# The four token stages of layer 0 run as one pipeline instead of four fenced stages

## The reference

```python
x = L0_attn_hidden_states                      # 4 batches x 2048 tokens x 256
x = x + 0.5 * _L0_ffn_ref(_layernorm(x), ...)  # layer 0
x = x + _L0_attn_ref(_layernorm(x), ...)
x = x + 0.5 * _L0_ffn_ref(_layernorm(x), ...)  # layer 1

# _L0_ffn_ref, per token
logits = flat @ router_w.T
topk_scores, topk_idx = jax.lax.top_k(logits + router_bias, TOPK)   # TOPK = 2
topk_scores = jax.nn.softmax(topk_scores, axis=-1)
hidden = jax.nn.silu(gate_all) * up_all        # 16 experts
out = jnp.einsum('nk,nkd->nd', combine, down_all)
sh_hidden = jax.nn.silu(flat @ sh_gate.T) * (flat @ sh_up.T)
out = out + sh_hidden @ sh_down.T
```

## Time and profile before

| | us |
|---|---|
| median of 3 runs | 2016.77 |
| lowest and highest of them | 2015.26 and 2021.91 |
| the profiled execution, whole | 2013.89 |
| its span in the trace | 2012.2 |
| PE busy, share of the span | 1480.4, 74% |
| DVE busy, share of the span | 1047.0, 52% |
| POOL busy, share of the span | 876.3, 44% |

### The profile page before, as it was taken

How to read it: one execution, slowest core, us unless ns; L and a number is a source line. 1 busy time by engine, 2 the same in 40 slices (tenths; PEclk the granted TensorE clock), 3 DMA queues, 4 the chain that set the end, 5 groups by cost and what they waited for, 6 DMA issues and landing times.

```text
span 2012.2 us, 35562 instructions
## 1 busy us (share of the span) xinstructions
PE 1480.4 (74%) x11274; PEld 1247.8 (62%) x11275; DVE 1047.0 (52%) x3253; ACT 617.5 (31%) x1254; POOL 876.3 (44%) x1108
## 2 busy tenths in 40 slices
PE   4797787999967779578767779698674447799650
PEld 3787677988854548455654559587543327698540
DVE  4657546544434755556734766243553547474332
ACT  2333223444423323233212323244321103244220
POOL 4563486655532200210272006655135463756656
PEclk9897798999976889688877889799786767799775
DMA  4732224556541122210231021356223352256555
GB/s 116 225 104 65 84 79 126 167 164 157 161 136 43 48 74 74 81 39 24 90 121 43 27 74 63 107 160 156 84 64 110 105 157 77 87 156 176 147 146 170
DMA packets 166002, 215.71 MB, mean 107 GB/s; under 512 B 18800, under 2 KB 143856, under 8 KB 165872
## 3 DMA queue, kind: packets, MB, share of 16 engines
q0 software_dynamic: 32256, 90.22, 17.0%
q1 hardware_dynamic: 87920, 79.74, 12.3%
q10 hardware_dynamic: 45696, 44.05, 6.6%
HBM read 119.56 MB, written 94.37 MB: 106 GB/s over the span
## 4 chain that ended last, share of the span: by engine, by line
PE 53%; DVE 14%; POOL 13%; issue 10%; DMA 4%; ACT 4%; another core or an unknown queue 2%; ACTq 0%; DVEq 0%; POOLq 0%; SPq 0%
PE bank L1444 8%; PE bank L1455 7%; PE bank L1594 7%; PE bank L1457 6%; PE bank L1456 6%; PE bank L1515 4%; DMA out<-normalised_rows 3%; POOL queries_high L739 2%; POOL normalised_rows L655 2%; POOL gathered_last_results L655 2%; DVE bn_stats L1042 2%; POOL rows_and_results L722 2%; PE bank L1846 2%; DVE score_maxima L1328 2%
## 5 line engine op out<-in xcount | busy, mean ns | idle before, releaser
L722 POOL DMA_INDIRECT rows_and_results<-normalised_by_token,rows_of_slots x336 | 319.7, 952 | 215.4 <-PE bank L1444 131.5
L655 POOL DMA_INDIRECT gathered_results<-slot_results,slot x128 | 122.0, 953 | 389.4 <-DVE combined_rows L1278 282.8
L1226 DVE TENSOR_TENSOR rows_transposed_low<-bank,rows_transposed_high 128x512 fp32r<-128x512 f32 x168 | 116.0, 691 | 270.2 <-ACT rows_transposed_high L812 178.6
L1455 PE MATMUL bank<-expert_gate_up_high,rows_transposed_high 128*128 x672 | 210.3, 313 | 47.1 <-DVE rows_transposed_low L1226 27.1
L737 POOL TENSOR_SCALAR keys_high<-iota,place_in_page_of_choice 128x128 fp32r<-128x128 f32 x96 | 57.6, 600 | 330.1 <-DVE place_in_page_of_choice L1165 322.7
L1456 PE MATMUL bank<-expert_gate_up_low,rows_transposed_high 128*128 x672 | 194.3, 289 | 0.0
L1457 PE MATMUL bank<-expert_gate_up_high,rows_transposed_low 128*128 x672 | 194.1, 289 | 0.0
L1594 PE MATMUL bank<-expert_down,hidden_work 128*128 x672 | 186.6, 403 | 0.5
L1455 PEld LDWEIGHTS bank<-expert_gate_up_high,rows_transposed_high 128*128 128x128 f32 x672 | 132.8, 198 | 60.0 <-issue 58.5
L1455 PE MATMUL bank<-rows_transposed_high,shared_gate_up_high 128*128 128x256 f32 x512 | 159.1, 311 | 0.3 <-DVE hidden_work L1001 0.3
L1444 PE MATMUL bank<-identity,hidden_work 128*128 128x128 f32 x464 | 96.8, 308 | 78.0 <-ACT hidden_work L766 29.8
(11 more groups left out here) (277 smaller groups left out, 3754.9 us busy)
## 6 DMA issues: line engine op xcount, KB each, us to landing
slot_results<-rows_and_results ACTq DMA_DIRECT2D x168, 256.0 KB
partial_sums<-rows_and_results SPq DMA_DIRECT2D x96, 256.0 KB, 2.1
rows_and_results<-partial_sums SPq DMA_DIRECT2D x72, 256.0 KB, 4.3
normalised_by_token<-normalised_rows SPq DMA_DIRECT2D x64, 256.0 KB, 2.5
rows_and_results<-in_L_attn_hidden_states SPq DMA_DIRECT2D x32, 256.0 KB, 3.3
normalised_rows<-partial_sums POOLq DMA_DIRECT2D x24, 256.0 KB
out<-normalised_rows POOLq DMA_DIRECT2D x24, 256.0 KB, 2.7
rows_and_results<-normalised_by_token,rows_of_slots POOLq DMA_INDIRECT x336
```

The source lines that it names most:

```text
L655: gp.indirect_dma_start(into[:, t, k, :], None, ys[part], bass.IndirectOffsetOnAxis(ap=slot[:, b, k, 2 * i + t:2 * i + t + 1], axis=0))\
L722: gp.indirect_dma_start(rows[:, i % NS, t, :], None, norm_d, bass.IndirectOffsetOnAxis(ap=listed[:, page:page + 1], axis=0))\
L1226: dve.tensor_tensor(flat(xt_l[:, k]), bank[k][:], flat(xt_h[:, k]).bitcast(F32), ALU.subtract)\
L1455: pe.matmul(out_, lh, rh, start=first, stop=False)
```

## The change

Stages 1 to 3 become `chained`. Their engines no longer wait at a fence. The stage before them (`ph["next"]`) issues the first work of the next batch inside its own last turns: statistics and norm of pairs 0 and 1 on DVE at turn 6, `apply` of both pairs on ACT at turns 7 and 8, `turn` of pair 0 on PE and `high` on ACT at turn 8, `low` of pair 0 and the norm of pairs 2 and 3 on DVE at turn 9. A chained stage has three norm groups instead of two. The third one (pairs 4 to 7) stands at its turn 2.

The slot computation of a batch moves too. Its chunks stand at turns 0, 2, 3, 4 and 5 of the stage; in stage 3 chunk 3 stands at turn 3. `list_slots` of the stage's slots is left to turn 3 of the following stage, with the last 14 of 32 `invert` matmuls in that stage's turns 0 to 3. Only stage 3 still ends with its own list. The ranks go to `bank[1]` instead of `bank[5]`, so `turn(3)` has to wait for the two DVE operations that read them. SP loads a pair of the next batch one turn earlier.

```diff
@@ the phases
+            ph["chained"] = bool(ph["kind"] == "T" and ph["n"] and phases[ph["n"] - 1]["kind"] == "T")
+            ph["next"] = phases[ph["n"] + 1] if ph["kind"] == "T" and phases[ph["n"] + 1]["kind"] == "T" else None
+        def groups_of(ph):
+            return ((0, 2), (2, 4), (4, PB)) if ph["chained"] else LN_GROUPS[ph["kind"]]
@@ SP, tokens
-                    if after["kind"] == "T" and i >= 2:
-                        load_when_stored(i - 2)
+                    if after["kind"] == "T" and i >= 1:
+                        load_when_stored(i - 1)
@@ ACT, tokens
-                apply(0)
-                apply(1)
+                if not ph["chained"]:
+                    apply(ph, 0)
+                    apply(ph, 1)
                 for i in range(PB + 1):
-                    if i < PB:
-                        high(i, i % NS)
+                    if i < PB and not (i == 0 and ph["chained"]):
+                        high(ph, i)
+                    if i == PB and ph["next"]:
+                        high(ph["next"], 0)
                     if i:
-                        tanh(i - 1, (i - 1) % NS)
+                        tanh(i - 1)
                     if i + 2 < PB:
-                        apply(i + 2)
+                        apply(ph, i + 2)
+                    if i >= PB - 1 and ph["next"]:
+                        apply(ph["next"], i - PB + 1)
@@ DVE, tokens
                 for i in range(PB + 2):
-                    if i < PB:
-                        low(i, i % NS)
-                    if i == 0:
-                        for n in range(5, PB):
-                            rows_statistics(n)
-                        layer_norm(ph, 2)
-                    if hosted and i < ROUTE_CHUNKS:
-                        next(hosted)
+                    if i < PB and not (i == 0 and ph["chained"]):
+                        low(ph, i)
+                    if i == PB + 1 and ph["next"]:
+                        low(ph["next"], 0)
+                    if ph["chained"]:
+                        if i == 0:
+                            next(hosted)
+                        if i == 2:
+                            next(hosted)
...
+                    if ph["chained"]:
+                        if i in (1, 2):
+                            rows_statistics(ph, 2 + 2 * i)
+                            rows_statistics(ph, 3 + 2 * i)
+                        if i == 2:
+                            layer_norm(ph, 4)
+                        if i == 3:
+                            next(hosted)
+                            if listed_late:
+                                list_slots(listed_late)
+                        if i == (4 if ph["next"] else 3) or i == 5:
+                            next(hosted)
+                    if ph["next"]:
+                        if i == PB - 2:
+                            rows_statistics(ph["next"], 0)
+                            rows_statistics(ph["next"], 1)
+                            layer_norm(ph["next"], 0)
+                        if i == PB:
+                            weight_differences()
+                            rows_statistics(ph["next"], 2)
+                            rows_statistics(ph["next"], 3)
+                        if i == PB + 1:
+                            layer_norm(ph["next"], 2)
@@ PE, tokens
+                    if i == 3 and ph["chained"]:
+                        r = ph["hosts"]
+                        pe.wait_ge(route.sem, r["route"] + ROUTE_PICKED + ROUTE_RESET * r["start"] + 2)
...
+                    if i == PB and ph["next"]:
+                        turn(ph["next"], 0)
+                    if i == 2 and ph["chained"]:
+                        pe.wait_ge(tr_low.sem, tr_low.done(ph["t"] + 1))
+                        ranks(ph["hosts"], bank[1])
...
+                    if listed_late and i < 4:
+                        invert(listed_late, INVERTED_LATE[i], INVERTED_LATE[i + 1])
...
+INVERTED_CHAINED = (0, 0, 3, 8, 13, 18, 18)
+INVERTED_LATE = (18, 18, 23, 28, 32)
+INVERTED_LAST = (0, 0, 4, 9, 14, 20, 32)
@@ every engine, at the start of a phase
-                fence(pe, "pe", ph["n"])
+                if not ph["chained"]:
+                    fence(pe, "pe", ph["n"])
```

More of the change, by code:

```diff
@@ L540, in _ @@
                     load_tokens(ph, range(NS))
+                if ph["chained"]:
+                    tokens(ph)
+                    continue
                 if ph["n"]:
@@ L1033, in tokens @@
                         choose(i - 1, (i - 1) % NS)
[L1034 to L1037 removed]
+                    if ph["chained"]:
+                        if i in (1, 2):
[8 more added lines that the diff above has]
+                        if i == (4 if ph["next"] else 3) or i == 5:
+                            next(hosted)
+                    if ph["next"]:
[9 more added lines that the diff above has]
+                            layer_norm(ph["next"], 2)
+                if not ph["next"]:
+                    if hosted:
+                        list_slots(ph["hosts"])
+                    weight_differences()
                 dve.drain().then_inc(phase_done["dve"].sem, 1)
@@ L1429, in _ @@
             for ph in phases:
-                fence(dve, "dve", ph["n"])
+                if not ph["chained"]:
+                    fence(dve, "dve", ph["n"])
                 {"T": tokens, "E": experts, "C": combine, "A": attention}[ph["kind"]](ph)
@@ L1517, in down_ @@
                     m.then_inc(dn_pe.sem, 1)
+                listed_late = phases[ph["n"] - 1]["hosts"] if ph["chained"] else None
+                inverted_by = INVERTED_BY if not ph["chained"] else INVERTED_CHAINED if ph["next"] else INVERTED_LAST
                 for i in range(PB + 2):
-                    if i < PB:
-                        turn(i, i % NS)
+                    if i < PB and not (i == 0 and ph["chained"]):
+                        turn(ph, i)
+                    if i == PB and ph["next"]:
[3 more added lines that the diff above has]
+                        ranks(ph["hosts"], bank[1])
                     if 1 <= i <= PB:
@@ L1525, in tokens @@
                         down_(i - 2, (i - 2) % NS)
+                    if listed_late and i < 4:
+                        invert(listed_late, INVERTED_LATE[i], INVERTED_LATE[i + 1])
                     if ph["hosts"]:
-                        if i == 1:
-                            ranks(ph["hosts"])
+                        if i == 1 and not ph["chained"]:
+                            ranks(ph["hosts"], bank[5])
                         if i >= 4:
-                            invert(ph["hosts"], INVERTED_BY[i - 4], INVERTED_BY[i - 3])
+                            invert(ph["hosts"], inverted_by[i - 4], inverted_by[i - 3])
                 pe.drain().then_inc(phase_done["pe"].sem, 1)
```

70 lines of the change are left out of this document (38 added, 32 removed).

## The result

The changed kernel takes 1998.97 us in the median of four runs (1992.5 to 2000.01), the kernel before 2016.01 us in the median of four (2014.29 to 2021.91). The ratio is 0.9911, with a 95% interval of 0.9893 to 0.993. The forecast was 2000 us.

The account below looks back on a forecast made before the run. PE was taken to set the pace over most of the span, with some 20 us per stage filling and draining. Gains of 30.9 us less 6.5, 4.5 and 5.6 gave 14.3, forecast 2000 us, range 1987 to 2014.

Parts of the forecast that it names:

- the mark: Start of ACT's exponential that waits for stage 3's list; the wait was forecast to end near 286 us.
- the three costs: Stage 0 with its crossing 6.5 us, builds beside norms and chunks 4.5, falls of PE's clock 5.6.
- Clean pipeline: Rival: short stalls leave the clock high, builds don't touch DVE; gain 20 to 28 us, 1987 to 1994; chance 0.20.
- The stage laid out on paper: A chained stage takes 57.6 us between last silus; stage 1 gains 10.4 us, stage 2 gains 13.7.
- Stage 3: POOL's 32 builds set its end, 77.8 us after stage 2's last silu; gain 6.8 us.
- Stage 0: Added statistics and a norm of 5.4 us lose 4 us inside, 2.5 more at the crossing to stage 1.
- Builds beside the norm: POOL's builds stretch norms to 3.6 us at six places, and chunks 0 to 2 of stages 2 and 3: 4.5 us.
- The rival in which DVE waits for each build: A norm takes 7.4 us; the kernel becomes 14 us slower than before, near 2028; chance 0.07.
- The clock: PE falls to 1.2 GHz after stalls of some 3 us: two falls in three stages, 2.8 us each, 5.6 in all.
- My sign for it: More than three stretches of granted clock 0.5 in stages 1 to 3 would price the clock higher.
- The sum: Clean gain 30.9 us less costs of 6.5, 4.5 and 5.6 makes 14.3 us.
- The signs: Last silus of stages 0 to 3 near 81, 140, 200 and 259 us, with 58 to 62 us between them.

Follow-up runs that it names:

- the yardstick: The changed kernel run once more, unchanged, on the second chip: 1993.73 us, ratio 0.988 to the kernel before.
- e9: Changed kernel, but in stage 3 POOL does the first 22 of 32 builds and DVE the last 10: 1996.94 us, ratio 0.9849 to the kernel before.
- e4: Changed kernel, but POOL fills the low halves of the expert weights by one-input copies, not subtractions: 1994.87 us, ratio 0.9852 to the kernel before.
- e3: Changed kernel with the inversions of stages 1 and 2 one turn later: 1993.13 us, ratio 0.9891 to the kernel before.
- e8: Changed kernel with the inversions of stages 1 and 2 and the third norm each one turn later: 1989.41 us, ratio 0.9855.
- e5: Changed kernel with fences back and no next-batch work begun early; late list, moved chunks and three norm groups kept: 2021.72 us, ratio 0.9986.

## Why the prediction was right

The time was right to about 1 us, and so was the mark (286 forecast, 286.71 measured). That is closer than the steps deserve, since two of the three costs were mis-sized in opposite directions, and so it is partly luck. On the second chip the same change saves 22.9 us (ratio 0.988), more than the 17 forecast and at a time, 1993.7, that I had given to the rival *Clean pipeline*, though the clock falls there as well. (That rival's gain was added up wrongly: 5 to 10 us less of costs make 19 to 24 us, not 20 to 28.)

- **The stage laid out on paper.** Clean, it was 57.6 us for gaps of 11.8, 3.6, 10.9, 4.5 and then 26.8. Stage 2 after has 11.8, 3.7, 10.7, 7.8 and then 30.4 (5.9, 11.4, 6.4, 6.7), 64.4 in all. The first three gaps are right to 0.2 us each, with the queue order and durations of the earlier trace rows alone. That each of them fits is luck, since the yardstick has 11.7, 5.2 and 9.1; that their sum fits isn't, 26.3 on paper against 26.2 and 26.0, and 26.9 in stage 3. In stage 1 it is 29.9. Pair 3 is too slow by 3.3 us and pair 5 by about 5, of which 1.7 is waiting for the builds; behind these lie the two stretches at 1.2 GHz, some 3.3 us each.
- **Stage 3.** Its end is set by POOL, as forecast: 78.6 us from the end of stage 2's last silu, where I had 77.8. e9 shows it directly, since giving a third of the builds to DVE moves the list by 7.4 us while the silus stay. The clock's fall from 236 to 241 costs nothing here: DVE works without a pause from 234.51 until chunk 3 is done at 242.6.
- **Stage 0.** The 4 us inside the stage were 5.7 at its last silu; a fall of the clock (78 to 81) stands in front of it. The 2.5 at the crossing show in stage 1, whose first three gaps are 3.6 us over the lay-out. The norm took 5.1 us for a forecast of 5.4 (5.5 by the last row). e4 takes this cost away and ends stage 0 at 77.1.
- **Builds beside the norm: the wrong term.** I took 4.5 us, with a norm of 3.6 at six places. Builds stand beside only four norms of stages 1 to 3. These take 3.0 to 3.4 us, the one from 134.61 to 137.87 3.3, hardly above the 2.9 of the earlier trace rows: 1.3 us together. The third groups take 3.0 us each, with twice the elements and no build beside them, and a chunk under builds grows by 0.2 us (chunks 0 and 1 of stage 3). So the term should have been about 2. The rival in which DVE waits for each build is refuted: the small operations below run at 0.15 to 0.25 us, with a build under way at each moment, and the longest one of a norm beside builds takes 0.31.

```profile
134.61 0.25 DVE L1109 TENSOR_TENSOR mean_difference<-bn_stats 128x4 f32<-128x4 f32 x1
134.78 0.15 DVE L1110 TENSOR_TENSOR mean<-bn_stats 128x4 f32<-128x4 f32 x1
...
136.65 0.16 DVE L1127 SCALAR_TENSOR_TENSOR rsqrt_steps<-rsqrt_steps,variance 128x4 f32<-128x4 f32 x1
...
137.71 0.16 DVE L1132 SCALAR_TENSOR_TENSOR minus_mean_by_deviation<-mean,rstd 128x4 f32<-128x4 f32 x1
```
```profile
134.48 0.60 POOL L745 TENSOR_SCALAR keys_high<-iota,place_in_page_of_choice 128x128 fp32r<-128x128 f32 x1
...
136.66 0.64 POOL L745 TENSOR_SCALAR keys_low<-iota,place_in_page_of_choice 128x128 fp32r<-128x128 f32 x1
```

The Trainium skill, page "SBUF — State Buffer", section "SBUF: two separate sides", describes an exclusive lock between the two engines. By this trace it holds for POOL's casts and subtractions and doesn't for its builds, a comparison with a scalar from each partition. The Trainium skill makes no such difference there among operations that read SBUF; the measurement decides.

- **The clock: the other wrong term.** I counted two falls of 2.8 us, 5.6 in all. Stage 2 alone has two that cost some 3.3 us each. The first profile has four in stages 1 and 2 (89 to 91, 96 to 102, 171 to 177 and 188 to 194), besides one in stage 0, and one in stage 3, where POOL's builds hide it. The fall at 171 stands where I had looked for one, near pair 3. The one that I hadn't thought of stands at pair 5, where PE waits for the first builds behind chunk 3. The lay-out counted `invert` at its own length and no wait for its inputs. e3 shows that this wait goes with one constant. My sign for it, more than three stretches at 0.5 in stages 1 to 3, came: there are five.
- **The sum.** Above the clean lay-out, stages 1 and 2 lie by 61.4 - 57.6 = 3.8 and by 64.3 - 57.6 = 6.7 us, 10.5 together, where my costs for them (2.5, 4.5 and 5.6) make 12.6. Stage 3 misses 0.7 of its gain. Stage 0 loses 5.7 instead of 4. So 30.9 - 10.5 - 0.7 - 5.7 = 14.0, against 14.3.
- **The signs.** The last silus of stages 1 to 3 came at 143.44, 207.76 and 267.00, not near 140, 200 and 259, and stage 2 is 64.3 us long, not 58 to 62. These signs were wrong beside the forecast itself: 286 less the 77.8 of stage 3 puts stage 2's last silu at 208, where it is. PE, not DVE, fills pairs 4 to 7: from 183.66 to 208.14 it is busy for 22.6 us and DVE for 14.7.
- **The part of the run behind the mark** gave nothing back, as expected.

What stays open is why the clock falls in one execution and not in another at the same stall. And e3 and e8 bring 10 and 13 us at the mark, by one profile each, but 0.6 and 4.3 in the medians. Part of it may be the place of the falls in the profiled executions; how much of it is lost behind the mark these runs don't tell.

## What to carry to other kernels

A crossing between two batches is as short as the longest thing left between the last work of one and the first of the other on the busiest queue. The late list without the early start and the early start without the late list brought nothing, both with a fence 6 us at the mark, and both without it 14. Count the clock into such a stop: a stall of 4.7 us at the fence cost another 3.2 us of slower matmuls behind it. Lay such a stage out from the durations of the trace in queue order: it gave the first three pairs of stage 2 right to 0.3 us in the sum, and missed the waits for operands that another engine has yet to build and the falls of the clock. When a stage ends in a row of short operations on the slow engine while a fast one waits for them, give it the last third: 13.7 us of waiting became 0.8.

## What the runs showed of the hardware

- DVE's two-input operations waited for POOL's cast (0.62 us, until its end) as well as for its subtraction (1.11), but not for its comparisons with a scalar: 0.15 to 0.31 us each beside these.
- The clock fell to 1.2 GHz for about 6 us after stalls of only 0.78 and 0.90 us in one execution, and not after 0.64 and 0.94 us at the same place in another.
- The kernel before had medians of 2016 and 2024.5 us on different chips. In the traces of the changed kernels the part behind the token stages takes 1706 to 1715 us on one of the faster chips and 1716.5 to 1721 on the slower ones (but for the 1729 of e5), which is about that difference.
- Behind a stall of 4.71 us at the fence the gate and up matmuls of a pair took 6.9 us at a granted clock of 0.5, against 3.7 us at 1.0 where there was no such stall.
